# Expert weights copied through internal DRAM before they are split, and the parts of q and k stored once and repeated on load

## What is computed

```python
x = L0_attn_x                                   # [8, 512, 128]
x = layernorm(x + attention(x))                 # 16 heads of size 8, causal, softmax
x = layernorm(x + experts(x))

# experts, T = 4096 tokens, E = 64 experts of inner width 64
scores = sigmoid(x @ router_w.T)
sfc = scores + e_bias                           # chooses 4 of 8 groups, then 8 experts
coef = chosen scores / their sum * 2.5          # [T, E], 0 where not chosen
g = einsum('th,ehi->tei', x, Wg); u = einsum('th,ehi->tei', x, Wu)
h = silu(g) * u * coef[:, :, None]
out = einsum('tei,eih->th', h, Wd) + (silu(x @ SWg) * (x @ SWu)) @ SWd
```

## Time and profile before

| | us |
|---|---|
| three runs | 955.06, 957.02, 960.02 (median 957.02) |
| profiled execution, span from the first to the last instruction | 952.6 |
| TensorE busy | 932.2 |
| VectorE busy | 750.5 |
| GpSimd busy | 598.4 |
| ScalarE busy | 462.6 |

### The profile page before, as it was taken

One profiled execution on the slowest core, in us unless ns is written; L12 is line 12 of the kernel. 1 busy time (PEld: TensorE's weight loads), 2 busy tenths in 40 slices (PEclk: granted clock), 3 DMA queues, 4 the chain that ended last, 5 costly groups with the idle time before them and its releaser, 6 DMA issues.

```text
span 952.6 us, 16050 instructions
## 1 busy us (share of the span) xinstructions
PE 932.2 (98%) x5008; PEld 581.8 (61%) x5008; DVE 750.5 (79%) x2374; ACT 462.6 (49%) x866; POOL 598.4 (63%) x651
## 2 busy tenths in 40 slices
PE   8899999999999999999999999999999999999996
PEld 3355566666666666666666666675666666666664
DVE  5776887799877997799967997699967996578664
ACT  3355455455555545555555545555545555533221
POOL 2342247775777657775767757776667767775653
PEclk9799999999999999999999999999999999999998
DMA  8552154334534253433534254242633323242431
GB/s 292 159 167 67 50 176 146 113 104 136 181 96 135 92 184 126 136 114 96 192 115 136 84 179 138 94 136 73 211 117 113 114 88 95 87 162 82 138 129 56
DMA packets 64340, 121.70 MB, mean 128 GB/s; under 512 B 6656, under 2 KB 36224, under 8 KB 63744
## 3 DMA queue, kind: packets, MB, share of 16 engines
q1 hardware_dynamic: 64256, 120.67, 39.6%
HBM read 98.37 MB, written 22.02 MB: 126 GB/s over the span
## 4 chain that ended last, share of the span: by engine, by line
PE 85%; DVE 9%; issue 2%; DMA 2%; ACT 1%; SPq 0%; POOL 0%; POOLq 0%; DVEq 0%; ACTq 0%
PE acc L879 12%; PE ob L820 7%; PE sm L790 7%; PE st L808 7%; PE pu L749 6%; PE pg L749 5%; PE pg L751 5%; PE pg L750 5%; PE pu L750 5%; PE pu L751 5%; PE acc L745 4%; PE acc L864 2%; PE acc L866 2%; PE acc L865 2%; PE ob L832 2%
## 5 line engine op out<-in xcount | busy, mean ns | idle before, releaser
L993 POOL TENSOR_TENSOR hid<-hid,coef_b 128x512 f32<-128x512 f32 x240 | 309.5, 1290 | 134.7 <-DVE hid L1250 106.0
L1182 DVE CUSTOM_DVE_ANT_0 max_out<-sm,causal_sb 128x128 bf16<-128x128 f32 (+3 forms) x512 | 236.1, 486 | 60.6 <-PE sm L790 58.6
L942 ACT ACTIVATE hid<-pg 128x512 f32<-128x512 f32 x243 | 145.3, 598 | 245.2 <-PE pg L751 236.6
L914 ACT ACTIVATE probs<-st 128x512 f32<-128x512 f32 (+1 forms) x384 | 192.5, 525 | 75.8 <-PE st L808 74.1
L1241 DVE SCALAR_TENSOR_TENSOR hid<-hid,pg 128x512 f32<-128x512 f32 x243 | 165.8, 682 | 51.1 <-ACT hid L942 50.8
L997 POOL TENSOR_TENSOR hid_lo<-hid,hid_hi 128x512 fp32r<-128x512 f32 x112 | 144.0, 1285 | 75.7 <-ACT hid_hi L949 75.3
L1250 DVE TENSOR_TENSOR hid<-hid,pu 128x512 f32<-128x512 f32 x235 | 160.3, 682 | 30.0 <-PE pu L751 27.8
L979 POOL TENSOR_SCALAR_AFFINE_SELECT probs<-probs 128x256 f32<-128x256 f32 x256 | 97.8, 408 | 75.3 <-ACT probs L914 75.3
L790 PE MATMUL sm<-k_stack,q_stack 72*128 72x128 bf16 (+3 forms) x512 | 132.8, 307 | 3.7 <-DMA k_stack<-k_rows_dram 1.9
L749 PE MATMUL pg<-x_hi,wg_hi 128*128 128x512 f32 x240 | 127.7, 532 | 0.3 <-DVE hid L1241 0.2
L808 PE MATMUL st<-q_stack,k_stack 96*128 96x512 bf16 (+3 forms) x512 | 125.9, 304 | 0.2
(11 more groups left out here) (161 smaller groups left out, 1295.4 us busy)
## 6 DMA issues: line engine op xcount, KB each, us to landing
coef_b<-coef_dram SPq DMA_DIRECT2D x128, 512.0 KB, 3.9
q_rows_dram<-qk_parts SPq DMA_DIRECT2D x24, 384.0 KB, 4.1
k_rows_dram<-qk_parts SPq DMA_DIRECT2D x24, 384.0 KB, 3.5
q_stack<-q_rows_dram SPq DMA_DIRECT2D x64, 144.0 KB
k_stack<-k_rows_dram SPq DMA_DIRECT2D x64, 144.0 KB
xT_sb<-in_xT SPq DMA_DIRECT2D x8, 256.0 KB, 3.8
y<-in_x SPq DMA_DIRECT2D x8, 256.0 KB, 3.9
out<-out_sb SPq DMA_DIRECT2D x8, 256.0 KB, 2.6
```

Of the source, the lines that this page charges most:

```text
L914: act.activation(probs[:, h % HG, at:at + wide], st_bank[i % 2][:, 0:wide], ACT.Exp, scale=C ** -0.5).then_inc(exp_done, 1)
L942: act.activation(hid_of(n, i), gate_bank(n, i)[:, :], ACT.Tanh, scale=0.5).then_inc(tanh_done, 1)
L993: pool.tensor_tensor(hid_of(n, i), hid_of(n, i), coef_b[:, half % 2, j, :], ALU.mult)\
L1182: last = dve.tensor_tensor_reduce(out=max_out[:, seg.nth(BANK_SM, task) % 2, col:col + wide], in0=sm_of(seg, task)[:, col:col + wide], in1 ...
```

## The change

Raw chunks no longer go from the inputs to a spare place on the chip. Task `wcp` copies a chunk from the input to a new DRAM tensor, task `wld` waits for that copy and loads it into the place of its own low part, and the split is done in that place, all 11 chunks on ScalarE and GpSimd. TensorE gets waits for the low parts (`G_CHUNKS`, `D_CHUNKS`), ScalarE loses its wait at the first exponent. The parts of q and k are stored once; a stack load is three DMAs for q and one for k, whose sources repeat rows. Key blocks 1 and 3 change places in `probs`.

```diff
-SPLIT_BY_DVE = 3
-CHUNKS = 9
+CHUNKS = 11
+STACK_LOADS = 4
+G_CHUNKS = {0: 1, 1: 3, 9: 6, 17: 8, 25: 11}
+D_CHUNKS = {1: 4, 17: 9}
-KB_AT = (0, 512, 1024, 896)
-ST_PARTS = ((0,), (1, 3), (2,))
+KB_AT = (0, 640, 1024, 512)
+ST_PARTS = ((0,), (3, 1), (2,))
 WEIGHTS = {
-    "wld": (-64.01188, -52.11215, -47.6205, -47.46299, -43.9597, -41.25746, -39.6625, -37.09062, -28.57236,),
-    "chunk": (-56.67708, -47.11707, -46.76868, -44.70277, -41.27095, -41.0331, -35.30701, -33.30581,
-        -24.97616,),
+    "wcp": (-60.1, -58.1, -56.1, -54.1, -52.1, -50.1, -48.1, -46.1, -44.1, -42.1, -40.1,),
+    "wld": (-58.0, -56.0, -54.0, -52.0, -50.0, -48.0, -46.0, -44.0, -42.0, -40.0, -38.0,),
+    "chunk": (-54.3, -50.3, -46.3, -42.3, -38.3, -34.3, -32.3, -30.3, -28.3, -26.3, -24.3,),
 }
-    q_rows_dram = nc.dram_tensor("q_rows_dram", [2, PARTS, PARTS, C, NH, S], BF16).ap()
+    q_rows_dram = nc.dram_tensor("q_rows_dram", [2, PARTS, C, NH, S], BF16).ap()
...
+    gu_raw_dram = nc.dram_tensor("gu_raw_dram", [2, P, E * I], F32).ap()
+    wd_raw_dram = nc.dram_tensor("wd_raw_dram", [P, PAIRS // 2 * D], F32).ap()
+    sgu_raw_dram = nc.dram_tensor("sgu_raw_dram", [P, 2 * P], F32).ap()
...
+        narrow = E * I // 4
+        chunks = [(SWgu, sgu_raw_dram, sgu_hi[:, :], sgu_lo[:, :])]
+        for part in range(4):
+            cols = slice(part * narrow, (part + 1) * narrow)
+            chunks.append((Wg[:, cols], gu_raw_dram[0, :, cols], wg_hi[:, cols], wg_lo[:, cols]))
+            chunks.append((Wu[:, cols], gu_raw_dram[1, :, cols], wu_hi[:, cols], wu_lo[:, cols]))
+            if part % 2 == 0:
+                cols = slice(part // 2 * narrow, (part // 2 + 1) * narrow)
+                chunks.append((Wd[:, cols], wd_raw_dram[:, cols], wd_hi[:, cols], wd_lo[:, cols]))
...
-                dst = q_rows_dram[par, p] if kind == "q" else k_rows_dram[par, :, p]
-                sp.dma_start(dst.rearrange("o c h t -> (c h) o t"),
-                             qk_parts[:, kind == "k", p, :].unsqueeze(1).to_broadcast([P, PARTS, S]))\
+                dst = q_rows_dram[par, p] if kind == "q" else k_rows_dram[par, p]
+                sp.dma_start(dst.rearrange("c h t -> (c h) t"), qk_parts[:, kind == "k", p, :])\
                     .then_inc(parts_stored, 16)
...
+                    if kind == "wcp":
+                        sp.dma_start(chunks[i][1], chunks[i][0]).then_inc(raw_copied[i], 16)
                     if kind == "wld":
-                        place = chunks[i][4]
-                        if i - 2 >= SPLIT_BY_DVE:
-
-                            sp.wait_ge(lo_done, i - 2 - SPLIT_BY_DVE + 1)
-                        sp.dma_start(chunks[i][3], chunks[i][0]).then_inc(split_in[place], 16)
+                        sp.wait_ge(raw_copied[i], 16)
+                        sp.dma_start(chunks[i][3].bitcast(F32), chunks[i][1]).then_inc(raw_in[i], 16)
...
-                        for stack, dram in ((q_stack, q_rows_dram), (k_stack, k_rows_dram)):
-                            sp.dma_start(stack[0:QK_ROWS, 2 * j:2 * j + 2, :],
-                                         dram[par, :, :, :, hs].rearrange("a b c h t -> (a b c) h t"))\
-                                .then_inc(stacked[j], 16)
+                        for a in range(PARTS):
+                            rows = slice(a * PARTS * C, (a + 1) * PARTS * C)
+                            sp.dma_start(q_stack[rows, 2 * j:2 * j + 2, :].rearrange("r h t -> r (h t)"),
+                                         q_rows_dram[par, a, :, hs].rearrange("c h t -> c (h t)").unsqueeze(0)
+                                         .to_broadcast([PARTS, C, 2 * S])).then_inc(stacked[j], 16)
+                        sp.dma_start(k_stack[0:QK_ROWS, 2 * j:2 * j + 2, :].rearrange("r h t -> r (h t)"),
+                                     k_rows_dram[par, :, :, hs].rearrange("b c h t -> (b c) (h t)").unsqueeze(0)
+                                     .to_broadcast([PARTS, PARTS * C, 2 * S])).then_inc(stacked[j], 16)
...
                     if kind == "g":
+                        if n == 0 and i in G_CHUNKS:
+                            pe.wait_ge(lo_done, G_CHUNKS[i])
...
                     if kind == "chunk":
-                        _, hi, _, place, at = chunks[i]
-                        act.wait_ge(split_in[at], 16 * sum(c[4] == at for c in chunks[:i + 1]))
-                        act.activation(hi, place, ACT.Copy).then_inc(hi_done, 1)
+                        _, _, hi, lo = chunks[i]
+                        act.wait_ge(raw_in[i], 16)
+                        act.activation(hi, lo.bitcast(F32), ACT.Copy).then_inc(hi_done, 1)
...
-                    if kind == "chunk" and i >= SPLIT_BY_DVE:
-                        _, hi, lo, place, _ = chunks[i]
+                    if kind == "chunk":
+                        _, _, hi, lo = chunks[i]
                         pool.wait_ge(hi_done, i + 1)
-                        pool.tensor_tensor(lo, place, hi.bitcast(F32), ALU.subtract).then_inc(lo_done, 1)
+                        pool.tensor_tensor(lo, lo.bitcast(F32), hi.bitcast(F32), ALU.subtract).then_inc(lo_done, 1)
...
-                        for diagonal in (blocks[:, 0:5:4, :], blocks[:, 7:9, :]):
+                        for diagonal in (blocks[:, 0:5:4, :], blocks[:, 5:9:3, :]):
...
-                    if kind == "chunk" and i < SPLIT_BY_DVE:
-                        _, hi, lo, place, _ = chunks[i]
-                        dve.wait_ge(hi_done, i + 1)
-                        dve.tensor_tensor(lo, place, hi.bitcast(F32), ALU.subtract).then_inc(waiting_free, 1)
```

More of the change, by code:

```diff
@@ L434, in build @@
     out_tok = out.rearrange("(b t p) d -> b p t d", t=NT, p=P)
-    q_rows_dram = nc.dram_tensor("q_rows_dram", [2, PARTS, PARTS, C, NH, S], BF16).ap()
-    k_rows_dram = nc.dram_tensor("k_rows_dram", [2, PARTS, PARTS, C, NH, S], BF16).ap()
+    q_rows_dram = nc.dram_tensor("q_rows_dram", [2, PARTS, C, NH, S], BF16).ap()
+    k_rows_dram = nc.dram_tensor("k_rows_dram", [2, PARTS, C, NH, S], BF16).ap()
+    gu_raw_dram = nc.dram_tensor("gu_raw_dram", [2, P, E * I], F32).ap()
+    wd_raw_dram = nc.dram_tensor("wd_raw_dram", [P, PAIRS // 2 * D], F32).ap()
+    sgu_raw_dram = nc.dram_tensor("sgu_raw_dram", [P, 2 * P], F32).ap()
     coef_dram = nc.dram_tensor("coef_dram", [2, E, S], F32).ap()
@@ L553, in build @@
         id_in = sem("id_in")
-        split_in = [sem(f"split_in{j}") for j in range(5)]
+        raw_copied = [sem(f"raw_copied{j}") for j in range(CHUNKS)]
+        raw_in = [sem(f"raw_in{j}") for j in range(CHUNKS)]
         hi_done = sem("hi_done")
         lo_done = sem("lo_done")
-        waiting_free = sem("waiting_free")
         zero_done = sem("zero_done")
@@ L560, in build @@
         const_done = sem("const_done")
-        wide, narrow = E * I // 2, E * I // 4
-        waiting = probs[:, :, :].rearrange("p h c -> p (h c)")
-        coef_flat = coef_b[:, :, :, :].rearrange("p a j t -> p (a j t)")
-        chunks = [(SWgu, sgu_hi[:, :], sgu_lo[:, :], hid[:, 0, 0:2 * P], 0),
-                  (Wg[:, 0:wide], wg_hi[:, 0:wide], wg_lo[:, 0:wide], waiting[:, 0:wide], 1),
-                  (Wu[:, 0:wide], wu_hi[:, 0:wide], wu_lo[:, 0:wide], waiting[:, wide:2 * wide], 2)]
-        for src, hi, lo, parts in ((Wg, wg_hi, wg_lo, (2, 3)), (Wu, wu_hi, wu_lo, (2, 3)), (Wd, wd_hi, wd_lo, (0, 1))):
-            for part in parts:
-                cols, half = slice(part * narrow, (part + 1) * narrow), part % 2
-                chunks.append((src[:, cols], hi[:, cols], lo[:, cols],
-                               coef_flat[:, half * narrow:(half + 1) * narrow], 3 + half))
+        narrow = E * I // 4
[7 more added lines that the diff above has]
+                chunks.append((Wd[:, cols], wd_raw_dram[:, cols], wd_hi[:, cols], wd_lo[:, cols]))
         assert len(chunks) == CHUNKS
@@ L682, in tasks @@
                             if seg.nth(("rs",), ("rs", n - 2, j)):
-                                sp.wait_ge(stacked[j % RING_PAIRS], 16 * 2 * ring_nth(seg, n - 2, j))
+                                sp.wait_ge(stacked[j % RING_PAIRS], 16 * STACK_LOADS * ring_nth(seg, n - 2, j))
                         after(sp, seg, part1_done, ("q", "k"), task)
@@ L785, in tasks @@
                         if i % (3 * 2) == 0 and seg.nth(("rs",), ("rs", n, h // 2)):
-                            pe.wait_ge(stacked[h // 2 % RING_PAIRS], 16 * 2 * ring_nth(seg, n, h // 2))
+                            pe.wait_ge(stacked[h // 2 % RING_PAIRS], 16 * STACK_LOADS * ring_nth(seg, n, h // 2))
                         col = 0
@@ L863, in tasks @@
                             after(pe, seg, low_done, ("lo",), ("lo", n, i))
+                            if n == 0 and i in D_CHUNKS:
+                                pe.wait_ge(lo_done, D_CHUNKS[i])
                             pe.matmul(acc[:, :], wd_hi[:, w], hid_hi[:, :], start=first, stop=False)
@@ L904, in tasks @@
                         after(act, seg, st_full, ("st",), task)
```

(2 more changed lines are left out.)

## The result

The changed kernel takes 1097.55 us in the median (1095.08 to 1099.96, four runs), against 956.71 for the kernel before on the same chip: a ratio of 1.1471 [1.144, 1.1503], 141 us slower. The forecast was 1008 with 1046 as the upper end, so the direction was right and the size was not. The profiled execution has a span of 1094.9 us.

A forecast was written before the change was run, and what follows sets the result against it. TensorE, busy 98% of the span, was the bound, in the head the data queue. Head 20, ring 18 and 10, coefficients 3, splits -1 and +1 gave +51 on 952.6, plus 4.4: 1008 us, range 985 to 1035, with rivals 968 to 1046.

The forecast's parts named there:

- Part 1: Head, SyncE's queue: copies and loads of the weights' detour stand ahead of stack 0, issued at about 28 us.
- the +20: Head's first stage up to pair 3: later by 20 us from detour and slower stack loads together, ends +7 and +32.
- rival (a): Stack loads stay on 12 engines: head +7 us, no ring waits, 969 us in all; chance 0.12.
- Part 2: Stack loads: repeated sources confine them to three DMA engines, 4.5 us a pair, 3.3 us extra.
- Part 3: Ring of four stacks: loads arrive after TensorE needs them, +18 us in batches 0 and 1, +10 us later.
- From batch 2 on: Later batches: stack loads fall short mainly at pair 0 of a batch, +10 us, ends 0 and 20.
- Two more issues of 0.3 us each: SyncE's extra stack-load issues, 0.3 us each, were to be hidden under the transfer.
- rival (b): TensorE's clock: five waits of some 3 us in batches 0 and 1 each bring slow stretches, +25 us, 1033; chance 0.12.
- rival (c): Coefficient loads come late on engines 0 to 2, so TensorE waits for GpSimd's products: +45 us, 1050; chance 0.08.
- Part 4: Weight splits moved to ScalarE and GpSimd: -1 us on VectorE, +1 at the masks; key-block exchange 0.
- (d): Faster: copies hardly load the engines and smaller stores speed the first stack, 953 us; chance 0.04.
- (e): Nothing to measure: both delays vanish in slack, 957 us; chance 0.04.

The follow-up runs named there:

- w_only: Changed kernel with parts stored three times and stack loads of 72 plain rows again, leaving only the weights' detour through DRAM; 985.13 us, ratio 1.0297.
- qk_only: Kernel before with q and k parts stored once and the four repeated stack loads, weights as before; 1087.7 us, ratio 1.1375.
- k_once: Kernel before with only k stored once and loaded by one transfer repeating 24 rows three times, q as before; 991.92 us, ratio 1.0386.
- k_once_wide: Kernel before with only k stored once, loaded by three plain transfers of 24 rows; 956.4 us, ratio 0.9995.
- both_wide: Kernel before with q stored once, k twice, and both stacks filled by six plain transfers of 24 rows; 963.88 us, ratio 1.0072.
- mt_act: Changed kernel with the row-maxima load issued by ScalarE on its own queue instead of by SyncE; 1074.9 us, ratio 1.123.
- slow_issue: Kernel before with three tiny DMAs of 2 rows by 256 bytes between each q and k stack load; 980.58 us, ratio 1.0248.
- kb: Kernel before with only key blocks 1 and 3 exchanged in the probabilities; 956.91 us, ratio 1.0001.
- mt_first: Changed kernel with the row-maxima load put ahead of a stack load directly before it on SyncE; 1100.62 us, ratio 1.1524.

## Why the prediction was right in direction and too small

**Part 1, the queue of the first stage, was right in kind and nearly in size, less so in its division.** q's first part went at 15.64 (forecast about 14), stack 0 at 28.46 (28), used at 36.85 (34.4); stack 1 used at 47.46 (44.3), first exponent product 58.38 (56), pair 3 63.05 (60.5): +22.6 against +20. The price of a DRAM-to-DRAM copy, taken as a load's, held: with copies and loads in the queue 20 to 28 us ran at 371 GB/s and a share of 1.02. But the +20 hides how it was made. With wide loads it was to be +7 (rival (a)), the smaller stores' 4.7 already taken off: 11.7 for the detour alone, which leaves 8.3 for the other half. Pair 3 is late by 17.8 us in `w_only` (58.24) and by 6.7 in `qk_only` (47.11), by 22.6 together. So the detour was priced 6 us too low and the other half 1.6 too high, and the two overlap by 1.9. That the sum came so near is in part luck. Stacks 0 and 1 came 2.4 to 3.2 us later than forecast: issuing one took 3.1 us (28.46 to 31.56), where four issues of 0.3 had been assumed.

**Part 2, three engines, was right.** The share in a lone stack load is 0.18 and 0.13, and from issue at 64.22 to use at 71.54 it took 7.3 us (forecast 6.4). Rival (a), 12 engines, is out. `k_once` against `k_once_wide` shows by time that the shape is what costs.

**Part 3, the waits for stacks, was nearly right in sum**: 18.7 + 15.5 = 34.2 us against 18 + 10.

**The step that failed** is the treatment of a stack load as a delay to itself alone. "From batch 2 on ... +10 us (0 to 20)" counted the stack's own distance to its first matmul and set everything else against unused slack. What stands directly behind a stack on SyncE, the row-maxima load, was costed in the head only. In the trace of before it had no wait worth a row; with the stack's 2.9 us of issuing and its transfer on three engines ahead of a load that itself uses two of 16, it was late 20 times, 46.5 us, 40.2 of them in the expert phases (17 times and 37.4 us directly behind a stack). `k_once_wide` and `both_wide` (no row, and 1.8 us) show that this goes with the width, `mt_act` (8.4) that it goes with the queue. "Two more issues of 0.3 us each lie under the transfer" is the smaller error in the same place: about 0.7 each, and `slow_issue` prices that time at 24 us in a kernel with wide loads. The price could be read before: the earlier trace rows has 0.81 us for issuing the row-maxima load, whose outermost dimension is two. Of the 40.2 us in the expert phases issuing time alone makes 3.5 (`slow_issue`); what the narrow loads would make if their issue were fast no run shows (`k_once`, with one narrow load and one slow issue a stack, has 12.3 us over its span).

The Trainium skill, "DMA: Bandwidth & Descriptors", section "Why a DMA increments its semaphore by 16 and not by 1", also says that a hardware-queue transfer of k engines takes the lowest-numbered k. By that the maxima's two engines are always among the stack's three. The runs agree as far as they go: from issue to use this load took 4.0 to 5.9 us behind narrow stacks and 2.0 to 3.2 behind wide ones. They do not show engine numbers.

**The clock, rival (b), came as well**: 9.1 us from pair 3 to the first expert product and 25.1 in the expert phases. I had given it 25 us and the head only. The argument against, that TensorE is busy for over half of the time between waits, did not hold: slices fully busy after 2.3 and 3.8 us of waiting had 0.66 and 0.75. Not every wait did this (after 2.58 us at 532.34 the clock stayed at 1.00), but over the expert phases 59.9 us more of idle time came with 25.1 us of slower work, which multiplies whatever is missed. That the clock is a consequence of the waits is read from the windows (`both_wide` and `slow_issue` are at 1.00 from 560 to 670 us); no run separates it.

**Coefficients, rival (c)**: GpSimd's waits rose from 27.3 to 71.6 us and under 1 us of it reached TensorE in the changed kernel. It is real once the maxima are on time (28.3 in `mt_first`, 15.4 in `mt_act`).

**Part 4**: `kb` confirms the 0 for the key blocks. The splits' own share was not measured alone; it is inside `w_only`, where TensorE waits 3.0 us once, at 87.85, for masks that stand behind a split on GpSimd. The changed kernel's head has no such wait. The rivals (d), faster, and (e), nothing, are out.

Put together by the prediction's own terms: first stage 23 (20), stacks 34 (28), maxima 46.5 (0), clock 34 (0), the rest 4 (3): 142 against 51. Waits on narrow stack loads were the right mechanism, but not the larger part of the loss: 80 of the missing 91 us are the two terms that it had at nothing.

## What to carry to other kernels

A repeat in the slowest dimension of a DMA saves bytes, which were not short here, and gives up DMA engines, which were. Write the repeats as separate plain transfers: `k_once_wide` cost nothing. When a transfer gets slower, price everything that stands behind it, on its queue and on its engines, and not its own reader only; then price the clock for each new idle spell on TensorE. A wait moved in the queue is not removed: `mt_first` kept all of its time under two other names.

## What the runs showed of the hardware that was not expected

- The time that SyncE needs to issue a transfer goes with its shape. Medians: 0.31 and 0.36 us for the 72 rows of q and k (`before`), 0.36 for 24 rows (`both_wide`), 0.69 for an outermost dimension of 3 (the changed kernel), 0.70 for the row maxima's 2 (`before`), 0.57 for 2 rows of 256 bytes (`slow_issue`); 128 rows of SWgu took 0.43.
- Copies inside DRAM run as fast as loads: 371 GB/s at a share of 1.02 with both in the queue, and 374 at 1.05 in the same window of `w_only`.
- Waits of 2.3 and 3.8 us on TensorE were followed by 5 us at a granted clock of 0.66 and 0.75, one of 2.6 us by none below 1.00.
- The row maxima's load of 8 KB took 2.0 to 3.2 us from issue to use behind stack loads of 24 or 72 plain rows, and 4.0 to 5.9 behind the changed kernel's, which repeat rows in their outermost dimension.
